# A sorted tile's eight copies are issued by SyncE alone, in four pieces over several steps, with eight places for sorted rows instead of four; ScalarE issues copies for four tiles only

## The reference, cut to what matters

```python
edge_index = jnp.stack([src, dst])
xn = _layernorm(x, axis=-1)
x = x + _L0_gnn_ref(xn, edge_index, ...) + _L0_mix_ref(xn[None], ...)[0]
x = x + _L0_ffn_ref(_layernorm(x, axis=-1)[None], ...)[0]
...
logits = jnp.einsum('bsd,de->bse', xn, Wr) + br
top_vals, top_idx = jax.lax.top_k(logits, K)
w = jax.nn.softmax(top_vals, axis=-1)
w_full = jnp.einsum('bsk,bske->bse', w, jax.nn.one_hot(top_idx, E, dtype=w.dtype))
for e in range(E):
    h = jax.nn.gelu(jnp.einsum('bsd,dh->bsh', xn, W1[e]) + b1[e], approximate=False)
    y_e = jnp.einsum('bsh,hd->bsd', h, W2[e]) + b2[e]
    y = y + y_e * w_full[..., e, None]
```

## Time and profile before

| | us |
|---|---|
| median of 3 runs | 2243.01 |
| lowest and highest run | 2241.64, 2247.39 |
| span of the profiled execution | 2629.1 |
| PE, DVE, ACT, POOL busy in it | 1977.1, 1609.0, 1084.8, 1456.8 |

### The profile page before, as it was taken

One profiled execution on the slowest core, in us unless ns is written; L12 is line 12 of the kernel. 1 busy time (PEld: TensorE's weight loads), 2 busy tenths in 40 slices (PEclk: granted clock), 3 DMA queues, 4 the chain that ended last, 5 costly groups with the idle time before them and its releaser, 6 DMA issues. The chain is left out here.

```text
span 2629.1 us, 37526 instructions
## 1 busy us (share of the span) xinstructions
PE 1977.1 (75%) x9074; PEld 1396.6 (53%) x9075; DVE 1609.0 (61%) x3942; ACT 1084.8 (41%) x1932; POOL 1456.8 (55%) x1586
## 2 busy tenths in 40 slices
PE   8488887676766776766778777878888888898762
PEld 6365665554545554544555555555555666665431
DVE  7566666556666666586556665666765769553133
ACT  5322222234543443344545445555533655543110
POOL 3465656666666666655455555555565556530265
PEclk9788988887777777778888888898998998999876
DMA  9544544765555555545555555555556666531365
GB/s 319 142 133 132 141 123 116 221 185 143 160 153 144 156 151 148 151 129 148 147 167 158 149 153 142 150 149 146 146 152 165 163 166 160 155 109 59 116 194 168
DMA packets 286940, 401.66 MB, mean 153 GB/s; under 512 B 108852, under 2 KB 209492, under 8 KB 283199
## 3 DMA queue, kind: packets, MB, share of 16 engines
q0 software_dynamic: 74208, 206.08, 29.0%
q1 hardware_dynamic: 194348, 169.01, 21.9%
q10 hardware_dynamic: 18162, 24.08, 3.0%
HBM read 345.85 MB, written 81.96 MB: 163 GB/s over the span
## 5 line engine op out<-in xcount | busy, mean ns | idle before, releaser
L1534 POOL DMA_INDIRECT rows_g<-node_table,src_all x1347 | 1284.5, 954 | 922.1 <-issue 390.2
L2323 PE MATMUL psB<-rows_g,pick_e 128*128 128x260 f32 x2704 | 764.9, 441 | 111.7 <-issue 100.9
L2323 PEld LDWEIGHTS psB<-rows_g,pick_e 128*128 128x128 f32 x2704 | 589.6, 224 | 246.0 <-issue 141.7
L1709 DVE TENSOR_TENSOR rows_g<-rows_g,psD 128x2048 f32<-128x2048 f32 x169 | 384.9, 2277 | 0.0
L2122 ACT ACTIVATE pick_n<-local_row 128x1024 bf16<-128x1024 bf16 x169 | 178.6, 1057 | 389.6 <-remote 294.3
L1772 DVE COPY xn<-psD 128x256 f32<-128x256 f32 x112 | 47.4, 423 | 374.7 <-remote 143.7
L2364 PE MATMUL psC<-W_f,xnT 128*128 x448 | 246.3, 676 | 0.0
L2118 ACT ACTIVATE local_row<-local_row,minus_id 128x1024 bf16<-128x1024 bf16 x169 | 191.5, 1133 | 37.2 <-issue 25.2
L1680 DVE TENSOR_TENSOR pick_e<-psD,slot_all 128x1024 f32<-128x1024 f32 x169 | 203.8, 1206 | 0.1
L1556 POOL DMA_INDIRECT rows_g<-set_dram,places x98 | 96.2, 982 | 188.7 <-issue 165.3
L2312 PE MATMUL psA<-window,pick_n 128*128 128x24 bf16 x1352 | 61.2, 175 | 136.3 <-DVE psD L1690 49.8
(11 more groups left out here) (389 smaller groups left out, 3100.8 us busy)
## 6 DMA issues: line engine op xcount, KB each, us to landing
local_row<-local_dram SPq DMA_DIRECT2D x169, 256.0 KB
rows_g<-node_table,src_all POOLq DMA_INDIRECT x1347
xin<-sent_dram SPq DMA_DIRECT2D x112, 128.0 KB
set_dram<-xn SPq DMA_DIRECT2D x112, 128.0 KB
xnT<-in_xT_dram SPq DMA_DIRECT2D x96, 128.0 KB
sent_dram<-sorted_dram SPq DMA_DIRECT2D x96, 128.0 KB
sent_dram<-sorted_dram ACTq DMA_DIRECT2D x96, 128.0 KB
acc<-node_table SPq DMA_DIRECT2D x49, 128.0 KB
```

Of the source, the lines that this page charges most:

```text
L1534: pool.indirect_dma_start(out=rows_g[:, r, j], out_offset=None, in_=node_table, in_offset=bass.IndirectOffsetOnAxis(ap=src_all[:, g, j:j + ...
L1709: dve.tensor_tensor(heads, heads, p_here.unsqueeze(3).broadcast_to([P, EG, HEADS, C]), ALU.mult).then_inc(ph_ready, 1)
L2323: last = pe.matmul(ps_sum[s % 2][:, 0:AW], pick_e[:, s % SLOTS, j], rows_g[:, s % RING, j, 0:AW], start=(j == 0), stop=(j == EG - 1))
```

## The change

Tiles 10, 4, 1 and 0 are `RUSHED`: their set closes, or the next tile follows, soon after them. For these the copies of experts 0 to 3 are issued by SP in step `route_at[t] + 9` and those of experts 4 to 7 by ACT one step later, as before. For the other twenty tiles SP issues all eight copies, in four pieces of two copies (`BY_TWO`), and a list that is made when the kernel is built (`piece_at_step`) says in which step which piece goes: one piece a step, one or two in turn while more than four wait, and all that wait when a rushed tile comes. For tiles 23 to 11 this gives one and two pieces in turn in steps 84 to 119; for later tiles it is one piece in each of four steps. The sorted rows and `cuts` have eight places instead of four. Each piece has its own semaphore (`handed`), and a piece waits for the same piece of the tile before. Two semaphores instead of one count the stores of sorted rows. In an SP step, keeping a tile now stands ahead of handing out.

```diff
+SORT_BUFS = 8
+BY_TWO = 2
...
+    HANDS = NE // BY_TWO
+    RUSHED = tuple(t for t in SORTED if any(t == lo for _, lo in SETS[1:]) or route_at[max(t - 1, 0)] < route_at[t] + HANDS and t - 1 in (lo for _, lo in SETS[1:]))
+    piece_at_step, waiting = {}, []
+    for c in range(route_at[SORTED[0]] + 9, route_at[0] + 10):
+        waiting += [(t, k) for t in SORTED if route_at[t] + 9 == c and t not in RUSHED for k in range(HANDS)]
+        now = len(waiting) if any(route_at[t] + 9 == c for t in RUSHED) else 1 + c % 2 if len(waiting) > HANDS else 1
+        piece_at_step[c] = waiting[:now] + [(t, k) for t in RUSHED if route_at[t] + 9 == c for k in range(HANDS // 2)]
+        waiting = waiting[now:]
+    handed_at = {t: c for c, gone in piece_at_step.items() for t, _ in gone}
...
-    sorted_dram = nc.dram_tensor("sorted_dram", (4, 3 * P, D), F32).ap()
+    sorted_dram = nc.dram_tensor("sorted_dram", (SORT_BUFS, 3 * P, D), F32).ap()
...
-            cuts = sb("cuts", [1, 4, 2, NE], I32, c=ph)
+            cuts = sb("cuts", [1, SORT_BUFS, 2, NE], I32, c=ph)
...
-                    if n >= 4:
-                        sp.wait_ge(handed_low, handed_by(t + 4))
-                        sp.wait_ge(handed_high, handed_by(t + 4))
-                    sp.dma_start(sorted_dram[n % 4, 0:2 * P].rearrange("(k p) n -> p k n", p=P), sorted_home[n % 2][:]).then_inc(sorted_out, 16)
-
-                def hand_out(t):
+                    if n >= SORT_BUFS:
+                        for k in range(HANDS):
+                            sp.wait_ge(handed[k], handed_by(t + SORT_BUFS))
+                    sp.dma_start(sorted_dram[n % SORT_BUFS, 0:2 * P].rearrange("(k p) n -> p k n", p=P), sorted_home[n % 2][:]).then_inc(sorted_out[n % 2], 16)
+
+                def hand_out(t, k):
...
-                        sp.wait_ge(handed_low, handed_by(t + 1))
-                    for e in range(NE // 2):
+                        sp.wait_ge(handed[k], handed_by(t + 1))
+                    for e in range(BY_TWO * k, BY_TWO * (k + 1)):
...
-                            if max(table_at[x], route_at[SETS[x][1] + 1] + 10) == c:
+                            if max(table_at[x], handed_at[SETS[x][1] + 1] + 1) == c:
                                 fills(x)
...
                         for t in SORTED:
-                            if route_at[t] + 9 == c:
-                                hand_out(t)
                             if route_at[t] + 8 == c:
                                 keep_sorted(t)
+                        for t, k in piece_at_step.get(c, ()):
+                            hand_out(t, k)
...
-                    if n >= 4:
-                        dve.wait_ge(handed_low, handed_by(t + 4))
-                        dve.wait_ge(handed_high, handed_by(t + 4))
-                    dve.tensor_copy(cuts[:, n % 4, 0], off[0:1]).then_inc(cuts_ready, 1)
+                    if n >= SORT_BUFS:
+                        for k in range(HANDS):
+                            dve.wait_ge(handed[k], handed_by(t + SORT_BUFS))
+                    dve.tensor_copy(cuts[:, n % SORT_BUFS, 0], off[0:1]).then_inc(cuts_ready, 1)
...
-                        for t in SORTED:
+                        for t in RUSHED:
                             if route_at[t] + 10 == s:
-                                hand_out_rest(t)
+                                for k in range(HANDS // 2, HANDS):
+                                    hand_out_rest(t, k)
```

More of the change, by code:

```diff
@@ L1240, in loop_stage @@
                 "totals_done", "total_ready", "table_ready", "fills_out", "spare_out", "x1_out"))
-            pick_s_ready, cuts_ready, sorted_out, handed_low, handed_high, tails_out = (sem("s_" + n) for n in (
-                "pick_s_ready", "cuts_ready", "sorted_out", "handed_low", "handed_high", "tails_out"))
+            pick_s_ready, cuts_ready, tails_out = (sem("s_" + n) for n in ("pick_s_ready", "cuts_ready", "tails_out"))
+            sorted_out = [sem(f"s_sorted_out{u}") for u in range(2)]
+            handed = [sem(f"s_handed{k}") for k in range(HANDS)]
             ex_ready, share_ready = sem("r_ex_ready"), sem("r_share_ready")
@@ L1281, in handed_by @@
             def handed_by(t):
-                return 16 * NE // 2 * (sort_number(t) + 1)
+                return 16 * BY_TWO * (sort_number(t) + 1)
             def pair_tiles(e):
@@ L1355, in block_inputs @@
                         if x:
-                            sp.wait_ge(handed_low, handed_by(SETS[x][1]))
-                            sp.wait_ge(handed_high, handed_by(SETS[x][1]))
+                            for piece in range(HANDS):
+                                sp.wait_ge(handed[piece], handed_by(SETS[x][1]))
                         if filled_by(x):
@@ L1405, in hand_out @@
                     if n >= 1:
[L1406 to L1410 removed]
+                        sp.wait_ge(handed[k], handed_by(t + 1))
+                    for e in range(BY_TWO * k, BY_TWO * (k + 1)):
+                        frm = sp.value_load(cuts[0:1, n % SORT_BUFS, 0, e:e + 1], min_val=0, max_val=2 * P)
+                        to = sp.value_load(cuts[0:1, n % SORT_BUFS, 1, e:e + 1], min_val=0, max_val=NE * REGION - P)
+                        sp.dma_start(sent_dram[bass.ds(to, P)], sorted_dram[n % SORT_BUFS, bass.ds(frm, P)]).then_inc(handed[k], 16)
                 def pair_rows_in(k):
@@ L1426, in fills @@
                     if x:
-                        sp.wait_ge(handed_low, handed_by(SETS[x][1] + 1))
-                        sp.wait_ge(handed_high, handed_by(SETS[x][1] + 1))
+                        for k in range(HANDS):
+                            sp.wait_ge(handed[k], handed_by(SETS[x][1] + 1))
                     for e in range(NE):
@@ L1468, in on_sync @@
                                 sp.dma_start(sent_dram[NE * REGION + b * P:NE * REGION + (b + 1) * P], zero_dram).then_inc(spare_out, 16)
-                        for v in range(4):
+                        for v in range(SORT_BUFS):
                             if s == LAG + 3 + SPARE_F + v:
@@ L1850, in sort_out @@
                     then(dve.tensor_tensor(kinds[:, 1], counts_s[:, 0], off, ALU.add))
-                    if n >= 4:
-                        dve.wait_ge(handed_low, handed_by(t + 4))
-                        dve.wait_ge(handed_high, handed_by(t + 4))
-                    dve.tensor_copy(cuts[:, n % 4, 0], off[0:1]).then_inc(cuts_ready, 1)
+                    if n >= SORT_BUFS:
+                        for k in range(HANDS):
+                            dve.wait_ge(handed[k], handed_by(t + SORT_BUFS))
+                    dve.tensor_copy(cuts[:, n % SORT_BUFS, 0], off[0:1]).then_inc(cuts_ready, 1)
                     then(dve.tensor_scalar(kinds[:, 2], kinds[:, 1], float(-P), None, ALU.add))
-                    dve.tensor_copy(cuts[:, n % 4, 1], filled[0:1]).then_inc(cuts_ready, 1)
+                    dve.tensor_copy(cuts[:, n % SORT_BUFS, 1], filled[0:1]).then_inc(cuts_ready, 1)
                     then(dve.tensor_tensor(hit_s, chosen[:, u].unsqueeze(2).broadcast_to([P, 2, 3, NE]),
@@ L2175, in hand_out_rest @@
                     if n >= 1:
[L2176 to L2180, removed]
+                        act.wait_ge(handed[k], handed_by(t + 1))
+                    for e in range(BY_TWO * k, BY_TWO * (k + 1)):
+                        frm = act.value_load(cuts[0:1, n % SORT_BUFS, 0, e:e + 1], min_val=0, max_val=2 * P)
+                        to = act.value_load(cuts[0:1, n % SORT_BUFS, 1, e:e + 1], min_val=0, max_val=NE * REGION - P)
+                        act.dma_start(sent_dram[bass.ds(to, P)], sorted_dram[n % SORT_BUFS, bass.ds(frm, P)]).then_inc(handed[k], 16)
                 def take_sorted(half, t):
```

10 lines of the change are left out of this document (5 added, 5 removed).

## The result

The changed kernel takes 2190.2 us, the median of 4 runs from 2189.7 to 2191.6, against 2244.8 us of the kernel before on the same chip: a ratio of 0.9758, 95% interval 0.9744 to 0.9772. That is 54.6 us less, 2.4%.

The account below looks back on a forecast made before the run. No engine was full; waits of one engine on another paced the steps. Late 18.7 plus half the early 20.6 us, 29.0 us of profile, times 0.853 gave 25 us off 2243: 2218 us, range 2192 to 2258.

Parts of the forecast that it names:

- ScalarE relieved: Twenty tiles lose ACT's four copies, 5.83 to 11.68 us each: 117 to 234 us taken off ACT's queue.
- Only what others wait for is on the path: Of ACT's relieved time only DVE's waits behind hand-outs count, 39.3 us; PE's 49.2 us before line 2435 count as zero.
- Rival C: DVE's stalls delay PE, PE's the next pick: the full 39.3 and 24.6 us come back, 2188 us; chance 0.12.
- late 18.7 us: DVE's waits after 1690 us in lines 1805 and 1790, less tile 10's 7.48 us, counted in full as gain.
- early 20.6 us: DVE's waits before 1690 us in lines 1805 (13.6) and 1854 (7.0), counted half, 10.3 us.
- The price of a copy: One more copy on SP costs 2.31 us, so 52 early copies take 120 us.
- The room: SP's wait for ACT in line 1299, 97.9 us from 1219 to 1690, can absorb copies; 22 us too little.
- One factor of 0.853: 1 us of the profiled execution counts as 0.853 us of a plain run, assuming an even stretch.
- Smaller edits: Keeping before handing out, eight places, more semaphores and zero fills, shifted SP steps: taken as zero in all.
- Rival A: SP becomes the bound in the early stage: 2256 us at 3.03 us a copy, 2293 at 3.75; chance 0.18.
- Rival B: Nothing changes: the released engine meets the next wait in the same step, 2236 to 2249 us; chance 0.20.
- What would show it: Signs: lines 1805 and 1790 under 15 us, none in 1854, SP's wait near zero before 1690, about 50 after.

Follow-up runs that it names:

- x_early: Changed kernel with only tiles 23 to 11 relieved of ACT's copies; tiles 9 to 2 handed out half by ACT as before: 2198.7 us, ratio 0.9795.
- x_loads: Changed kernel plus 16 register loads and no copy on ACT in the old step of each of the 20 relieved tiles: 2266.2 us, ratio 1.0109.
- x_late: Changed kernel with only tiles 9 to 2, without 4, relieved of ACT's copies; tiles 23 to 10 half by ACT: 2241.2 us, ratio 0.9988.
- x_places: Changed kernel with its eight places, semaphores and SP order, but ACT keeps its half of every tile's copies: 2251.4 us, ratio 1.0034.
- second trace: The kernel before, unchanged, profiled once more: 2244.5 us, span 2242.7 us where the first trace spanned 2629.1.
- x_burst: Changed kernel, but SP issues all eight copies of a relieved tile in one step: 2225.0 us, ratio 0.9921.
- x_sploads: Changed kernel plus eight more register loads on SP behind each pair of copies of the relieved tiles: 2409.8 us, ratio 1.0750.
- x_actspread: Changed kernel's eight places, but ACT keeps its half of every tile and issues two copies a step instead of four: 2196.4 us, ratio 0.9793.

## Why the prediction was right or wrong, point by point

- **ScalarE relieved: right, and its price per hand-out too.** The prediction read 5.83 to 11.68 us from the first issue to the end of the fourth copy; undisturbed it is 6.1 to 6.9 in the stage, and 7.4 to 8.2 from the first register load on.
- **"Only what others wait for is on the path", searched by ACT's name: the step that failed.** I summed DVE's waits labelled ACT or standing at the lines right behind a hand-out, 39.3 us, and put PE's waits at zero. What a late ACT costs in the stage goes by way of PE, from the copy of line 2128 to PE's matmuls and to DVE's line 1772. Undisturbed, the waits that the sum looked for gave 7.5 us of the stage's 47.8 (5.0 for ACT, 2.5 for a place), and line 1772 gave 34.2. Its wait was the largest of DVE's in the 26 dense steps of the disturbed trace too, and PE waited for ACT there at two more lines (DVE's waits from 1309.6 to 1675.5, PE's from 1219 to 1690):

```profile
DVE xn L1772 <- PE psD L2416: 63.4, 6, 13.7
```

```profile
PE psC L2361 <- ACT hid L2138: 14.3, 5, 5.4
...
PE psA L2435 <- ACT xnT L2128: 9.3, 2, 7.3
```

  The sum left this wait out; of PE's stalls it named one row and counted it as zero. Rival C, all of the 39.3 and half of that row, gave 2188 us, within 2.2 us of the result, but that is partly luck: its 39.3 holds late 18.7 us that hardly came. Its reason, that DVE's stalls delay PE, is not the chain seen here either, in which a late ACT delays PE and PE delays DVE.
- **The early 20.6 us halved "because SP has no room": wrong.** It put 10.3 us, 8.8 of a run, where the stage lost 48.5. The price of a copy was good: 2.31 us a copy in that trace, 1.97 by the scale. One row after gives (6.49 - 0.54) / 3 = 1.98, and SP's lost wait of 161.9 us, less the 48.5 by which the stage shrank, over 52 copies 2.2. The room was not: 97.9 us in the earlier trace rows, 211.1 undisturbed. x_early has the early gain in full.
- **The late 18.7 us in full: wrong.** The 52 sparse steps lose 1.5 us. Line 1805, which stood with 16.2 us in that sum before tile 10's 7.48 were taken off, waits 6.1 us there undisturbed, and 4.0 after the change; DVE's wait for POOL's gathers, line 1698 before, takes up more than that difference. Line 1790, 10.0 us in that sum, has no wait for ACT there at all, only the one in the tail that is shown above. DVE's waits in these steps before, then after, and the busy time of the engines in them before:

```profile
DVE p_both_e L1698 <- DMA rows_g<-node_table,src_all: 17.7, 8, 4.7
...
DVE rr L1805 <- ACT std_r L2159: 6.1, 2, 3.5
```

```profile
DVE p_both_e L1710 <- DMA rows_g<-node_table,src_all: 22.1, 9, 4.1
...
DVE rr L1817 <- ACT std_r L2171: 4.0, 1, 4.0
```

```profile
1428.10:1969.30 541.20, 516.09 (x2774) 379.17 (x2773) 454.52 (x1082) 351.76 (x665) 388.84 (x408) 0.97 0.69 188
```

  ACT has (541.20 - 351.76) / 52 = 3.6 us left in each of them, about as in the stage, so by the sum above the six tiles relieved there should have brought some 20 us; why they bring 1.5 is open. The 16 loads of x_loads cost less there too: its 48 steps behind the stage take 503.2 us against 493.1, 10.1 for six tiles where 13 cost 57.6. That the gathers pace these steps would explain it, and was not tried. What was found late, 10.2 us of x_late against x_places, lies half in the tail.
- **One factor of 0.853: wrong in kind.** The prediction named it as an assumption, and its last sentence named this failure: the extra time of that execution did sit partly in queue instructions, SP's above all (906 us in all, against 815 in the second trace).
- **Smaller edits at zero: off by the 8.5 us of x_places** (2251.4 against 2242.8). No one place carries them (the stage has 2.7), and their cause is open.
- **Rival A** was not met, but is real: x_burst and x_sploads show SP as the bound as soon as its copies come in a lump or cost double. One of its figures was summed wrongly: at 3.75 us a copy its own terms give 52 us and 2288, not 59 and 2293.
- **Rival B** fell: DVE's waits for ACT went, and its wait for PE at line 1772 shrank, from 53.6 to 36.1 us, where B let it grow. The rule it named says that another issuing engine saves only time on the sequencer, usually small relative to the DMA itself (the Trainium skill, "DMA: Bandwidth & Descriptors", section "Issuing engines are not separate DMA queues"). That time was not small here: the same copies from another queue, two a step, are worth 2.4%. But x_actspread has all but 6 us of that on the old engine, so the engine was not the point.
- **What would show it**: lines 1805 and 1790 wait 5.8 us in these stretches after the change, and line 1854 not at all, as said; SP's wait fell to 49.2 us in the stage, not near zero, and to 122.2 in the steps behind it, not to about 50.

## What to carry to other kernels

Price instructions that hold up an in-order queue by the step: lump plus the engine's busy time in a step, less the step's length; what overruns can be on the path, and what fits costs little. Here 7.0 + 7.4 us in a step of 10.95. It is an estimate on the mean: it came near in the dense stage, and in the sparse steps it promised 20 us where 1.5 came. So before moving work to another engine, try to spread it on its own. And when summing what an engine's lateness costs, follow a wait back through the engine it is labelled with: the largest row stood under PE's name, and in the step followed above it began on ACT.

## What the runs showed that was not expected

One profiled execution was 17% longer than the plain runs (2629.1 against 2243.0 us), with the same medians of single instructions. The register loads of `cuts` on SP in the second trace, and the arithmetic behind those on ACT (count, ns min/median/max, first and last start):

```profile
L1408 SPq TENSOR_LOAD <-cuts x96: 262/270/457, 1037.9 to 2082.4; - x96
```

```profile
L2178 ACTq FUSED_REGOPS  x96: 147/147/162, 1053.9 to 2082.5; - x96
```

SP's median was 268 in the earlier trace rows and is 270 here, but its longest went from 902 to 457 ns, and ACT's arithmetic from 700 to 162. Medians were to be trusted there, idle times and sums of waits not: SP's room came out less than half. A span far above the plain runs says that every wait in it needs a second source.

Part of the gain goes with TensorE's clock. In the stage PE is busy 378.01 us before and 358.52 after for the same matmuls, at a mean granted clock of 0.92 and 0.97. Windows of before around the step shown above (PE's busy us first, the clock third from the end):

```profile
1202.00:1217.70 15.70, 11.69 (x61) 8.37 (x59) 13.08 (x23) 8.58 (x16) 11.95 (x13) 1.00 0.73 209
1217.70:1227.50 9.80, 8.90 (x31) 5.08 (x32) 0.00 (x0) 5.79 (x14) 2.23 (x3) 0.65 0.42 117
```

After PE's 4.07 us of waiting for ACT the clock is 0.65 of full speed on the mean of the next 9.8 us, between its levels of 1.2 and 2.4 GHz, and the eight matmuls take 3.78 us instead of 1.99. So this stall of PE was paid twice, once as waiting and once as slower matmuls behind it: those from line 2409 to line 2364 take 8.75 us in this step and 5.69 after, 3.1 of the 7.6 us by which the step shrank. How much of the 48.5 us of the stage is the one and how much the other was not separated: PE's busy time fell by 19.5 us.
